# One program per batch for projection and attention, and four moved schedules, in a two-layer transformer kernel

## The reference, cut to what matters

```
x = LN(x + attention0(x))   # 32 query heads, 8 key heads, head size 16, RoPE, causal
x = LN(x + ffn0(x))         # w_fc, w_proj rounded to -1, 0, 1 times mean |w|; inputs quantised
x = LN(x + attention1(x))   # linear: elu(q), silu(v), kv = elu(k)^T v, out = elu(q) kv,
                            # LayerNorm, times silu(u), times Wo
x = LN(x + ffn1(x))         # 16 experts of width 352, the top 2 of a softmax, plus a shared one
```

## Time and profile before

| | us |
|---|---|
| median of 3 runs | 1765.38 (1762.38 to 1768.72) |
| the profiled execution: its time, its span | 1765.3, 1763.5 |
| qkv0 / attn0 (to 84, to 355) | 84 / 271 |
| qkv1 / attn1 (to 418, to 690) | 63 / 272 |
| ffn (to 930) | 240 |
| lin (to 1120) / out (to 1233) | 190 / 113 |
| disp (to 1343) | 110 |
| sparse / moe (to 1658, to 1763) | 315 / 105 |
| busy over the span: PE, DVE, ACT, POOL | 90%, 67%, 53%, 33% |

### The profile page before, as it was taken

How to read it: one execution, slowest core, us unless ns; L and a number is a source line. 1 busy time by engine, 2 the same in 40 slices (tenths; PEclk the granted TensorE clock), 3 DMA queues, 4 the chain that set the end, 5 groups by cost and what they waited for, 6 DMA issues and landing times. The chain is left out here.

```text
span 1763.5 us, 33276 instructions
## 1 busy us (share of the span) xinstructions
PE 1592.7 (90%) x12554; PEld 804.8 (46%) x12554; DVE 1179.6 (67%) x2076; ACT 934.5 (53%) x1641; POOL 574.1 (33%) x581
## 2 busy tenths in 40 slices
PE   5799999887999987999987999787996999999997
PEld 3433333353333333344433445454564556666564
DVE  4499998556999964899866777796632243333387
ACT  5656677434677754777745565477231343333332
POOL 4555574262000021133221111496172111111265
PEclk9899999999999998999998999899998999999999
DMA  7322232000000001556547999552071764556344
GB/s 251 105 61 56 63 78 38 13 1 1 2 2 2 2 2 49 114 110 122 109 84 258 337 356 343 195 188 85 1 152 32 271 236 142 178 167 212 115 130 132
DMA packets 177841, 211.40 MB, mean 120 GB/s; under 512 B 114203, under 2 KB 117625, under 8 KB 175505
## 3 DMA queue, kind: packets, MB, share of 16 engines
q1 hardware_dynamic: 170336, 188.54, 35.5%
q0 software_dynamic: 7344, 20.73, 4.4%
HBM read 193.33 MB, written 56.40 MB: 142 GB/s over the span
## 5 line engine op out<-in xcount | busy, mean ns | idle before, releaser
L768 ACT ACTIVATE attn_prob<-attn_ps_t 128x512 f32<-128x512 f32 x576 | 312.5, 596 | 153.5 <-PE attn_ps_t L722 152.1
L800 DVE TENSOR_REDUCE attn_mx<-attn_ps_s 128x2 f32<-128x1024 f32 (+3 forms) x304 | 339.0, 1155 | 26.1 <-PE attn_ps_s L703 22.5
L2156 PE MATMUL sparse_ps_g<-wgate,sparse_xT 128*128 128x352 f16 x1128 | 186.6, 316 | 1.6 <-DVE sparse_xT L2234 1.6
L735 PE MATMUL attn_ps_o<-attn_prob,V 128*32 128x256 f32 x2304 | 175.4, 391 | 0.7 <-ACT attn_oT L776 0.7
L1273 PE MATMUL lin_ps_z<-arena,early 128*128 128x512 f16 x576 | 134.1, 384 | 10.4 <-DVE lin_relu L1421 7.0
L2156 PEld LDWEIGHTS sparse_ps_g<-wgate,sparse_xT 128*128 128x128 f16 x1128 | 109.3, 99 | 63.6 <-DVE sparse_xT L2234 2.1
L2240 DVE SCALAR_TENSOR_TENSOR sparse_hid<-sparse_th,sparse_ps_g 128x352 f32<-128x352 f32 x47 | 24.5, 521 | 152.6 <-ACT sparse_th L2201 152.6
L1033 PE MATMUL ffn_ps_y<-wprojT,ffn_hT 128*128 128x512 f16 x512 | 116.9, 388 | 8.0 <-DMA ffn_hT<-ffn_h 8.0
L2267 POOL DMA_INDIRECT xg<-x_d,token x45 | 42.5, 944 | 250.0 <-PE sparse_ps_x L2146 250.0
L703 PE MATMUL attn_ps_s<-KT,arena 64*128 64x512 f16 (+3 forms) x768 | 114.5, 332 | 10.4 <-DVE attn_mx L800 10.2
L1023 PE MATMUL ffn_ps_fc<-wfcT,early 128*128 128x512 f16 x512 | 114.3, 382 | 4.9 <-PEq L686 3.4
(11 more groups left out here) (311 smaller groups left out, 3144.4 us busy)
## 6 DMA issues: line engine op xcount, KB each, us to landing
wgate<-gate_d SPq DMA_DIRECT2D x47, 1408.0 KB
wdown<-down_d SPq DMA_DIRECT2D x47, 768.0 KB
lin_sp_raw<-in_L_ffn_w_gate_up_dram SPq DMA_DIRECT2D x56, 352.0 KB, 5.2
gate_d<-lin_sp_parts SPq DMA_DIRECT2D x56, 352.0 KB, 5.0
y_d<-y SPq DMA_DIRECT2D x47, 256.0 KB, 5.0
down_d<-lin_sp_parts SPq DMA_DIRECT2D x42, 256.0 KB, 5.6
lin_sp_raw<-in_L_ffn_w_down_dram SPq DMA_DIRECT2D x28, 256.0 KB, 5.0
wfcT<-in_L_ffn_w_fc_dram SPq DMA_DIRECT2D x8, 512.0 KB, 7.0
```

What stands on the lines that cost most here:

```text
L735: last = pe.matmul(ps_o[32 * jj:32 * jj + 32, 256 * half:256 * half + 256], V[:, kt, 4 * jg + jj, :], prob[(2 * q + jj // 2) % 4][:, half, ...
L768: act.activation(prob[g % 4][:, par, :, :], ps_t[:, (2 * g + par) % 3, :, :], ACT.Exp, scale=HD ** -0.5).then_inc(exp_done, 1)
L800: dve.tensor_reduce(mx[x % 2][:, c, :, at:at + per], ps_s[:, 2 * (r % 2):2 * (r % 2) + 2, 0:per * n].rearrange("p e (h k) -> p e h k", k=n ...
L2156: last = pe.matmul(ps_g[u][n][rows, :], xT[u][:, a, k, rows], w, start=(k == 0 and i == 0), stop=(k == KC - 1 and i == 2), skip_group_chec ...
```

## The change

1. `project_qkv` and `attend` become `attention_layer`, one block for each batch. The PSUM banks become one tile `banks` of 8: `ps_qkv`, `ps_v` and the second `ps_xt` lie where `ps_s` lies (0 to 3), `ps_q` and `ps_k` where `ps_t` lies (4 to 6), the first `ps_xt` and the sum at `ps_o` (7). SBUF scratch is shared too. The first FIRST = 4 events (s0, s1, m0, s2) are issued in the projection's last steps: on PE behind the turn of tile 6 and ahead of the turn of tile 7. New waits: s0 and s1 wait for the last RoPE and V copies (`rope_done`, `vals_done`), t0 and t1 for the copies of tile 7 (`qevac`, `kevac`).

```diff
-                unrolled(TB, [(1, of(xt)), (2, of(proj)), (3, of(tr)), (3, of(sums))])
+            def scores(t, u):
+                if t == TB - 1:
+                    attend_tensor(pe, ORDER[:FIRST])
+            unrolled(TB, [(1, of(xt)), (2, of(proj)), (3, of(tr)), (2, of(scores)), (3, of(sums))])
...
+                    if r < 2:
+                        pe.wait_ge(rope_done, TB)
+                        pe.wait_ge(vals_done, TB)
+                        pe.wait_ge(xt_evac, TB - ahead)
+                    if g < 2:
+                        pe.wait_ge(qevac, TB)
+                        pe.wait_ge(kevac, TB)
...
-                unrolled(TB, [(1, of(xevac)), (1, of(weights_low)), (2, of(rope)), (2, of(qlo)), (3, of(evac)), (3, of(threshold))])
+            unrolled(TB, [(1, of(xevac)), (1, of(weights_low)), (2, of(rope)), (3, of(evac)), (2, of(first_maxima)), (2, of(qlo)),
+                          (2, of(next_maxima)), (3, of(threshold))])
...
-                            project_qkv(nc, m, d, b, QT, KT, V)
-                            attend(nc, m, d, b, QT, KT, V)
+                            attention_layer(nc, m, d, b, QT, KT, V)
```

```diff
         dve.scalar_tensor_tensor(self.part(i, 1), self.raw[i % self.ring][0:rows, 0:width], WS, self.part(i, 0),
                                  ALU.mult, ALU.subtract).then_inc(self.lo_done, 1)
 
-    def spread(self, fn, eng, tiles):
-
+    def spread(self, fn, eng, tiles, later=0):
+
+
+        def until(t):
+            return self.count if t == tiles else max(0, t * self.count // tiles - later)
 
         def at(t):
-            for i in range(t * self.count // tiles, (t + 1) * self.count // tiles):
-                if t < tiles:
+            if t < tiles:
+                for i in range(until(t), until(t + 1)):
                     fn(eng, i)
         return at
 
...
-                              (1, split.spread(split.high, act, NT))])
+                              (1, split.spread(split.high, act, NT, 3))])
...
-                              (1, split.spread(split.low, dve, NT))])
+                              (1, split.spread(split.low, dve, NT, 3))])
```

3. In out, the orders of four engines change and the residual and what follows it comes one step later (first of PE, then ACT, DVE, POOL; `rows` on SP goes from lag 6 to 7):

```diff
-                unrolled(NT, [(4, wo), (3, wt), (0, q), (8, logit), (7, xt), (2, router)])
+                unrolled(NT, [(3, wt), (0, q), (8, xt), (9, logit), (4, wo), (2, router)])
-                unrolled(NT, [(2, whi), (6, xhi), (5, norm), (3, wevac), (2, split.spread(split.high, act, NT)), (7, xevac), (3, router)])
+                unrolled(NT, [(2, whi), (3, wevac), (6, norm), (6, xhi), (8, xevac), (2, split.spread(split.high, act, NT)), (3, router)])
-                unrolled(NT, [(1, gating), (4, residual), (0, stats), (8, levac),
+                unrolled(NT, [(5, residual), (1, gating), (0, stats), (9, levac),
-                unrolled(NT, [(2, wlo), (6, xlo), (1, product), (0, lambda t: ln_q.root(pool, t, t % 2)), (4, root_r)])
+                unrolled(NT, [(7, xlo), (2, wlo), (5, root_r), (1, product), (0, lambda t: ln_q.root(pool, t, t % 2))])
```

4. In disp, the parts of the tables move up and are put together; `tokens` goes from lag 2 to 1 and `scatter` from 8 to 6 (its four per step stay):

```diff
                     if t == 1:
                         softmax()
-                    if t == 2 or t == 3:
-                        choice(t - 2)
+                        choice(0)
+                    if t == 2:
+                        choice(1)
+                    if t == 3:
+                        running_sums()
+                        bases()
                     if t == 4:
-                        running_sums()
-                    if t == 5:
-                        bases()
-                    if t == 6:
                         slots()
-                    if t == 7:
                         owners()
...
                 def counts(t):
-                    if t == 4:
+                    if t == 3:
...
-                              (0, lambda t: half.gate_up(pe, t)), (1, counts), (2, tokens)])
+                              (0, lambda t: half.gate_up(pe, t)), (1, counts), (1, tokens)])
...
-                unrolled(NT, [(1, lambda t: half.low(pool, t)), (8, scatter)])
+                unrolled(NT, [(1, lambda t: half.low(pool, t)), (6, scatter)])
```

More of the change, by code:

```diff
@@ L674, in attend @@
             raw = [m.early[:, u * 4 * D:(u + 1) * 4 * D].bitcast(F32) for u in range(2)]
-            tern = [f.sb(f"tern{u}", [P, CHUNK], F16) for u in range(2)]
+            tern = [scratch[:, 5120 + u * CHUNK // 2:5120 + (u + 1) * CHUNK // 2].bitcast(F16) for u in range(2)]
             raw_in = [f.sem(f"raw_in{u}") for u in range(2)]
@@ L760, in _ @@
+                project_tensor(pe)
+                attend_tensor(pe, ORDER[FIRST:])
             @block.scalar
             def _(act):
[L762 to L789 removed]
```

966 lines of the change are left out of this document (495 added, 471 removed).

## The result

The changed kernel takes 1741.22 us, the median of 4 runs (1737.88 to 1745.59), against 1766.04 for the kernel before (4 runs, 1762.38 to 1768.72): a ratio of 0.986, interval 0.9839 to 0.9882, 24.8 us less. The forecast was 1744.1 within 1734 to 1757. A second set of 6 runs gave 1741.36 and a ratio of 0.9878 (0.9856 to 0.9900).

A forecast was written before the change was run, and what follows sets the result against it. PE is busy nine tenths of the span, so gains must come from its waits at block handovers and multi-engine stages. From 1765.3 us: layers -15.2, lin -1, out -3.5, disp -1.5, sum -21.2, giving 1744.1 us; range 1734 to 1757.

The forecast's parts named there:

- The layers, early scores: Projection/attention boundary: scores and maxima move into idle time, saving 7.9 us in batch 1, 7.4 in batch 0; together -15.2.
- held by ACT's copy of tile 6 and not by the scores: Batch 1's projection end: the turn of tile 7 starts at 413.44 as before, despite the scores ahead of it.
- Shifts as a whole: Layers, from the four maxima of s4 and after: the table keeps its old order and every engine's queue; only its time moves.
- the lock: Stage out: skill's exclusive lock on the port pair shared by DVE and GpSimd; L1630 took 1.71 us beside POOL's L1665.
- The -1: Lin: 1 us shorter, between +2 and -4.5; its start gains 4.5 us, but transfers set its end.
- the late release of the ring's buffers: Lin: three held pieces free their ring buffers later, so the loads behind them start up to 2 us late.
- the 5.5 of the working: Out: about 5.5 us of DVE work a tile remains once waits between engines go, down from 5.70.
- The case of no gain: Out: by the skill's lock rule, order alone wins nothing where both engines are full; this term would be 0.
- the 7.29 us at the turn of the table: Disp: PE's wait for the token table's read-back, claimed to go because the scatters end earlier.
- The second stall of 2.1 us: Disp: PE stalls 2.1 us behind slots and owners, 5.5 us of work joined in one step.
- that only the layers pay: Rival: lin, out and disp bring nothing, set by transfers, DVE with POOL, and stalls; 1752 us, chance 0.29.
- the slower rival: Out: residual and gating collide with POOL in every tile, 7.46 us instead of 5.70; 1780 us, chance 0.04.

## Why the prediction was right, and where it wasn't

- **The layers, early scores:** the mechanism is right. The working gave 7.9 us for batch 1; the trace has 9.3, of which 1.1 is the projection itself (from the first product to the turn of tile 7, 56.8 us before and 55.7 after). That the number came so near is in part luck of the clock: in six of eleven profiles it is 6.5, about the bound that the prediction gave (1.2 less) for a turn of tile 7 that still takes its old 2.7 us. For batch 0 it gave 7.4, and DVE's part (from the turn of tile 7 to the four maxima) fell from 12.9 to 5.1 us, 7.8. But that turn came 1.9 us later (81.63, not 79.77), so 5.9 was left. Here a step failed: "held by ACT's copy of tile 6 and not by the scores" was carried over to batch 0, and there the turn waited for the low parts on DVE (L774), which now stand behind the two maxima. The run without early scores parts boundary (1.6 and 2.0) and scores (4.0, and 4.5 to 7.3).
- **"Shifts as a whole":** this step failed. The queues kept their order, but POOL's chunks moved against DVE's, and the time of the eight small maxima fell from 7.1 to 3.4 us. That is 3.7 us of the 4.3 by which batch 0's body was shorter in the first pair, though profiles of this stretch at the higher and the lower granted clock differ by 2 to 3 us too. In the kernel before the waiting was 5.7 us in sum, and the run that takes it out is 4 to 5 us faster by the medians; in the changed kernel the same edit gains nothing that can be told. The sum of the prediction had no term for this. The prediction brought the lock up only for out; the earlier trace rows show one meeting of 512 columns, and I didn't look for short two-input instructions beside POOL's longest ones.
- **lin:** the start gained 3.9 us (4.5 told) and the end none, as told. The -1 has the wrong sign: lin became 2.2 us longer in the first profile, just over the bound of +2, and by the means of all profiles 1.6 us. Whether that is the late release of the ring's buffers, which the prediction named, no run shows.
- **out:** the tile went to 5.49, the 5.5 of the working, but that is luck: the step behind it failed. It had 5.5 us of DVE work a tile as a floor, and 0.2 us of waits for other engines that go. Over the 15 gaps DVE was busy for 5.05 us a tile before and 4.84 after, and idle for 0.65 both times. No idle time went in sum; the stretch of the earlier trace rows is only its densest part. The 3 us of the 15 gaps came, the 0.5 us at the ends did not, and eleven profiles make the whole 1.8 rather than 3.5. The case of no gain (both engines full, so order wins nothing) didn't come either, but little of the waiting at the lock went: in mid out the gating of the earlier trace rows went from 1.01 to 0.75 us in the mean, and the pieces that DVE splits from 0.98 to 1.17. Added up over the whole stage, what DVE's instructions took above the shortest of their kind is 9.4 us before, 8.7 after and 10.5 in the run with the old orders. How the rest of the gain comes about stays open.
- **disp:** stall by the sums and bases 4.50, as worked out, and the 7.29 us at the turn of the table went. The second stall of 2.1 us didn't come. And a term was missing: before, the sparse block started 3.6 us behind disp's last product, now 1.05. The second gather of its inputs had been issued at 1340.87, 1.7 us ahead of that product's end, and now at 1314.77, 4.4 ahead. That would explain it: in all three profiles with the tables in the old places the block starts 5.3 to 5.4 us behind this issue and 2.9 to 4.0 behind the product, and in the ten others that keep the loads in their place 1.05 behind the product. It wasn't tried by itself. Together the moved tables bring some 4.5 us in the mean rather than 1.5.
- **sparse** wasn't in the sum. Its first eight turns took 1.01 us before and 0.61 after, so it began at half clock there and at full clock here. But the kernels with old tables have 310.7 to 314.5 and those with new ones 310.4 to 314.8, so no gain of its own can be told.
- **The rivals:** that only the layers pay was wrong in disp and out by some 6 us, and the collisions of the slower rival didn't come, with gaps of 5.49 us and not 7.46.

The total was near (24.8 against 21.9 from the medians), by terms that were off by up to 4 us in both directions and cancelled in part: that is luck, and only the layers' early scores and the two waits of disp were understood as they came.

## What to carry to other kernels

When two programs meet at a boundary, look at what the consumer's first steps need: here three scores needed nothing of the last tile, and moving them into its wait gave over twice what removing the boundary gave. Where DVE and POOL both work, search for short DVE instructions with two SBUF inputs; one that takes ten times its usual length beside a long POOL instruction may be one that can be written with one input, as here. And read a stage's length from several executions, with the granted clock beside it, before a difference of 3 us is given a cause.

## What the runs showed that I had not expected

- A DVE instruction of 16 elements took up to 1.99 us (0.17 alone) beside POOL's 2.13 us instruction; as a one-input reduction it took 0.19 each of 16 times, beside the same POOL work. Beside a POOL instruction with one input (2.85 us) it was held only to 1.14 us behind that one's start.
- One program's executions differ by stage: 4.6 us in lin (transfers at 347 and 338 GB/s in its middle 144 us), 3.2 us in batch 1 (granted clock 0.83 and 0.67 in its first 10 us), and 11.8 us in disp with waits that no engine ended; while the totals of one kernel, in its fast executions, lie within 2 to 12 us of each other.
